# A two-layer decoder whose five engine queues are laid in a new order

## The reference, cut to what matters

```python
x = _layernorm(x + _L0_attn_ref(x, ...))           # a Mamba block: conv, silu, selective scan, gate
x = _layernorm(x + _L0_xattn_ref(x, ctx_768, ...)) # cosine similarity of two projections, 256 x 256
x = _layernorm(x + _L0_ffn_ref(x, ...))            # top-2 of 4 experts, low-rank additions to one MLP
x = _layernorm(x + _L1_attn_ref(x, ...))           # 16 heads, 4 key/value heads, rotary, softmax
x = _layernorm(x + _L1_xattn_ref(x, ctx_768, ...)) # one-head attention on the context
x = _layernorm(x + _L1_ffn_ref(x, ...))            # a gated recurrence over the 8 batches in turn
```

```python
h = dAt * h + dBxt                     # per batch, channel (512) and state (16), over 256 positions
y = jnp.einsum('bdn,bn->bd', h, Ct)
```

## Time and profile before

| | us |
|---|---|
| median of 3 runs | 1197.41 |
| lowest and highest | 1194.89, 1200.62 |
| the profiled execution | 1199.11 |
| span of its instructions | 1197.2 |

### The profile page before, as it was taken

The page is one execution under the profiler, slowest core; times in us unless marked ns, Lnnn a source line. Parts: engine busy times, 40 slices in busy tenths (PEclk is TensorE's granted clock), DMA queues, the critical chain, the costliest instruction groups (busy, mean ns, idle before and its releaser), DMA issues.

```text
span 1197.2 us, 17415 instructions
## 1 busy us (share of the span) xinstructions
PE 1083.9 (91%) x6154; PEld 794.0 (66%) x6154; DVE 1009.7 (84%) x1690; ACT 763.3 (64%) x2010; POOL 209.2 (17%) x257
## 2 busy tenths in 40 slices
PE   5666789899999999999998999999999999999984
...
DVE  3899999999999999999999999999998994333316
...
PEclk8766779999999999999999999999998999999997
...
GB/s 224 145 35 135 42 44 52 68 39 72 71 92 89 63 81 71 119 63 71 80 104 63 32 102 78 116 33 91 85 120 36 63 62 31 1 1 10 125 15 70
DMA packets 41193, 86.70 MB, mean 72 GB/s; under 512 B 3737, under 2 KB 14970, under 8 KB 40466
## 3 DMA queue, kind: packets, MB, share of 16 engines
...
## 4 chain that ended last, share of the span: by engine, by line
PE 67%; DVE 19%; issue 5%; ACT 5%; POOL 3%; DMA 1%; ACTq 0%; DVEq 0%; SPq 0%; POOLq 0%
PE bank L301 20%; DVE scans L598 5%; PE bank L716 5%; PE bank L1306 4%; PE bank L764 4%; PE bank L1344 4%; PE bank L1315 4%; PE bank L982 4%; PE bank L1355 3%; PE bank L974 3%; PE bank L532 3%; PE bank L1244 3%; DVE scans L606 2%; PE bank L1338 2%; PE bank L295 2%
## 5 line engine op out<-in xcount | busy, mean ns | idle before, releaser
L561 ACT ACTIVATE scans<-dt,a_neg 128x255 f32<-128x255 f32 x512 | 224.6, 501 | 0.1
L632 POOL DMA_DIRECT2D scans<-scans x96 | 84.6, 881 | 441.6 <-DVE scans L606 441.3
L606 DVE TENSOR_TENSOR scans<-scans,BC 128x1024 f32<-128x1024 f32 x128 | 155.9, 1218 | 0.2
L598 DVE TENSOR_TENSOR_SCAN scans<-scans 128x1024 f32<-128x1024 f32 x64 | 146.1, 2282 | 6.0 <-ACT scans L561 6.0
L598 DVE TENSOR_TENSOR_SCAN scans<-scans,dBx_odd 128x1024 f32<-128x1024 f32 x64 | 146.2, 2284 | 3.0 <-ACT scans L561 2.8
L1392 ACT ACTIVATE ya<-bank,nmax 128x256 f32<-128x256 f32 x240 | 110.7, 473 | 34.2 <-DVE nmax L1459 18.3
L532 PE MATMUL bank<-ident,scans 128*128 128x128 f32 x640 | 101.4, 296 | 18.0 <-DVE scans L606 17.7
L1459 DVE TENSOR_REDUCE nmax<-bank 128x2 f32<-128x512 f32 x128 | 84.3, 683 | 36.4 <-PE bank L1306 35.9
L532 PEld LDWEIGHTS bank<-ident,scans 128*128 128x128 f32 x640 | 82.5, 153 | 37.6 <-DVE scans L606 21.9
L1401 ACT ACTIVATE ya<-bank 128x512 f32<-128x512 f32 x120 | 68.6, 604 | 21.2 <-PE bank L1315 20.6
L1306 PE MATMUL bank<-kT,qT 64*128 64x256 f32 x512 | 72.3, 402 | 5.8 <-ACT ya L1401 4.5
...
## 6 DMA issues: line engine op xcount, KB each, us to landing
...
```

The source lines that it names most:

```text
L561: ins = act.activation(step[:, j, 1:S], dt[b % 2][:, c, 1:S], ACT.Exp, scale=a_neg[:, c, n:n + 1])
L598: dve.tensor_tensor_scan(H, H, flat(dBx[u % 2]), 0.0, ALU.mult, ALU.add).then_inc(s["a_scan"], 1)
L606: dve.tensor_tensor(H, H, Ch, ALU.mult).then_inc(s["a_hC"], 1)
```

## The change

Only the letters of `ORDER` change. Every engine keeps the same steps and each stream its own order, so the instructions, their operands and their semaphores are the same. The new strings come from a model of the queues in which a GpSimd instruction also waits for work with two SBUF operands that VectorE begins shortly behind it. How far the steps move: of DVE's 1294 steps 527 keep their place and 922 are within one place of it; of PE's 1245, 588 and 988; of ACT's 1155, 428 and 767; of POOL's 165 all but one are within one place, and of SP's 89 all but seven. The largest moves are two steps on ACT that come 36 and 44 places earlier. Of the pairs of DVE steps whose order turns round, 105 put an S step ahead of a W step and 84 one ahead of a Y step; 37 and 61 do the reverse.

In the start, DVE's order `F13 F14 S6 F15 S7 F16 S8 S9` becomes `F13 S6 F14 S7 F15 S8 F16 S9`. On ACT the two normalisations F16 and F17 stood ahead of S8 and now stand behind S9, and S10 to S15 are laid between F17 and F21. On PE, S4 and S5 now stand ahead of the turn F11, and W0 (four products) and S6 between F12 and F13. DVE's F17 moves from its 35th place to its 42nd. The step W5 of DVE (L1615 to L1617) stood ahead of S48 and now stands behind G1, so that G0 and G1 come before it.

In the middle, seven turns of a layernorm on PE (L295) now have other steps of PE ahead of them that stood behind:

| turn at, us | idle before it, us | now ahead of it |
|---|---|---|
| 266.84 | 0.40 | L1338 and L1344 (and L301 behind it) |
| 324.40 | 1.18 | L301 |
| 383.85 | 0.99 | L1306 |
| 476.35 | 1.43 | L1244, L532 |
| 635.44 | 0.66 | L1315, L301 |
| 653.82 | 0.24 | L1338, L1344, L532 |
| 900.01 | 1.60 | L1344 |

On SP, the load of batch 6's context for the second layer (`cz`, L946) moves from ahead of three loads of the scan's B and C (L501, `BC`) to behind them. PE's queue is the same from its 1190th step on.

```diff
     "pe": (
-        "FFFFFFFFFFSWFSSSFSFFYSYFFWSSSSYYSFSFSSFSYWSSSWGGGGSSFYSSWWWWWWYYSSYYWYWSWFSWFWWWFSYWWWWWYWWWWFFWWSWWWWYWWWWWSF"
-        "YYSWFYSYYYYSYYYYFYYSYYYSYYFYYSYSVYYGGVGGYSVSFYVFYWWWFYWWVSWVYSYYFFWVWYVYSYWVYVFWYSWWWYWVWFVYWYSWWYWVWSVWWFWSWY"
...
+        "FFFFFFFFFFSFSSSSSFFYWSFWYSSSFFSYSSFSSFYSSYWFSYGGGWGSSSFWWWYWSWYWYSSYWYSWSFWYFFWSWWWWWWSWWWWYWWFWWYFWWWWWSWWWWY"
+        "FYSFYSYYYYWYYYYFSYYYSYYFYYSYYYSSVVGGGYYGYFVVSFYYFWWWYWWSWVSYVYSYVVFWFYWYYWSYVYVWFSWWWYWVVWYSYWFWWYWWVSVWWFWWSW"
...
     "act": (
-        "FFFFFFFFFFFFFSSFSSSFFSSSFFSFSFFFSSSSSSFSSFFSSFSSSSSSFFSSSSSSSSGGWFSSSSSSGGWSWWSFSWWSWSWSFFFFSWSWSSWFFWWWSWFFSW"
...
+        "FFFFFFFFFFFFFSSFFSSSFSSSSSFFSSSFSFSFSFSSSSFSFFSSSSSFSSSSSSFFSSSGSGFWSSSGGSWWWSFSSSSSWWWSWFFSFFSSFWWFSWSWWSWWWF"
...
     "dve": (
-        "FFFFFFFFFFFFSWWSSSFSSFFSFSFSSSSSWSFSFYSFSSSSSSSFSYSSFSFSFSSSFSYWYSSSSSSSSSSSWSSSSFSWSGGSSGSGGFSGSGSGWSSYSSWYSS"
-        "WYWWSWYWWFYSSSWWWFWFWFWWSYWSWWYWSSSSWFYFSWSYFWSSSWFSSFSFYWFWFWSWYWYWSSSSSYYYSSSYSFYSSYSSFYYSSFSYYFYGGSFSYSSGFG"
...
+        "FFFFFFFFFFFWWFSSSFSSSFSFSFSFSSSSSSSSSYSSSFSSSFSSSWFSYSSFSFSFWSFFSSSSSYSSSSSSSSSFSWYSGGYWSGSGGFGSGSGWSSSSSSWYSS"
+        "WYWYWYWSWWFFSSSWFWFWYWYWSWSWSWWSWSWSYSSWFSSWFSWFSWSSFSYFWFFWFWYWYWWSSYSSSYYYSSYSFSFYSSYSSSYYSFFSYFYFSGGYSSGSGG"
...
     "pool": (
-        "FFGWWFWFGSSWWSSSSSSSSWWVSSSSWSSSSGFSWWSSSSSWWSVSSSSWSSSSSGFSWSWSSSSSSWWVSSSWSSSSSGSWSFWSSSSSSWWVSSSSWSSSGSSFWS"
-        "WSSSSSSWWSVSSSWSSSGSSWWSSSSSSSWWVSSSSWSSGWWWWVWWVWWWWWW"
+        "FFGWWFWFGSSWWSSSSSSSWSWVSSSSWSSSGSSFWWSSSSSSWWVSSSSWSSSSSGFSWSWSSSSSSWWVSSSWSSSSSGSWSFWSSSSSSWWVSSSWSSSSSGSFWS"
+        "WSSSSSSWWSVSSSWSSSGSSWWSSSSSSSWWSVSSSWSSGWWWWVWWVWWWWWW"
...
     "sp": (
-        "WFSFWSSFWSWGWSSFSFFWGSSSFFSSGWWWSWSSFFSGWWWWSSSFFSGWWWSSFWSSWGFWWSSFWSSWGWWWSSSGWWWWWWWWW"
+        "WFSFWSSWFSWGSFWSWSFFSGSSFFSSGWWWWSSFFSSWGWWSWSFSSFWGWWSSFSWSGFWWWWSSFSSGWWWSSSWGWWWWWWWWW"
```

More of the change, by code:

```diff
@@ L52 @@
[L52 to L56, removed]
@@ new lines @@
+        "FVYSWWWYFYFYVWVWWWWYYWWSYWSWYFWWVVWWFSWWYWWWWWWWSWWVVVVVVVVVSVYSFWYYWWYWYYWWYSWWYYWYSWYYSWYSWYWYWWWYWWSWWYWSYW"
+        "VYFSVWWGYYGGYGVVSYYSSSVYWVWWYYWYWWVFWVYSYFFYVVYWSYWYFFVVWWYYWWWYVWWVFWSYYWWFVVWWVSVWWVWWVWSWWWWWWWVWSVVVFSYWYY"
+        "SWWYWYYYWWSYWYWYYWYWSSYWWYWYWWWYSWWWWWSYYWVYSWWVGYGYGGYVVSSYSWFYWSWWYVVWYYWYVWVYSYYSVVFWYYWYFFWVVWYYSWWWWFWFWV"
+        "YVWWYSYWWVVWWSVFWWVFWVWWWSWWWWWVVVVSVYFYWSYWWYWYYWWYSWWYYYSWYWYYSWWYWYWWYWSWWWWWYSYWSWWGYVGGVGYYSSSFWYVVWWYWYY"
+        "SWWVWYVYSYVVFFFWYYWYVVSYWYSVYWFFWWWWVYWWYSWWVYVWWFWYWYSVVVWWVWWWFWSWWWWWSVVVVVVSYFWYYYWYWYSYWYWWYYWWYSWYWYSYWW"
@@ L59 @@
+        "WYWWSWWWYWWSWWSYWGWYGGGYSSWSFWVVWYWSYWYWWVVYYSYVVWWYWYSVYWVWWYWSWYWWYVVWSWYYWWYWWYVVWSYWWYWWWWVVYYWSWWWVVVVVSV"
+        "VVSVWVYWWYSYYYWYYYWWYSWWYYWSYWYWYYWSWYWWWWWWWWYSYWWSYVGGWGGVYYWYWWWVVYYWYWWVVYYYVVWYYWYVVWYYWVYVWWWWYYWWVYVWWY"
+        "YWWVVWWVVWWVWWWWWWWWWVVVVVYWYYYYYYYYYYWWYYWYYWYWYWYWYVVYWYYWVVYYWWYWVYYWWWWYVYWYWYVVYYYWWWWYVVWVVYYYVVYVVVVVVV"
         "WVVVWWWWWWWWWWWWWWWWWWWWWWWWWWWWWWW"
@@ L66 @@
[L66 to L70, removed]
@@ new lines @@
+        "WWWYWYVSYYFFSWFYWYWYYWSFVYSSWWVFYWSWYWSYSSFVSWWSSWWYWWSVVWWWSWWWWYSSWYWYWSSSSYYWWFWYWYSSWYSSYWYSYSYWSSYWGVYYGW"
+        "FYWYVYYGSGSWYYWYVYWWSFFYSYFYFSVYFSFYWWYWYYVWYFFYFSWSVYYFWWVYYWSYSFYWFWVSWSWSWSSSWWWWYSWWSVVWWWWSWYSWSWSYFYWWYW"
+        "YSSSSWWWYYWSWSYWYSYYSWYWWYGSYGSWYVYYGVGWSSYWYFSWWSYYYYVYYVYYSSFFYWWYWYYFFVWYFFSYWYSYVWWSFFSWYVYWYYFWFSSVWSFWWS"
+        "FSSWWSYWWFSWWVSVWWWWWSWWSYYSWWWSSYYYSWWYWSYWWSYSWWYSSWYWYGGWYSVYYSYSSWGGFYWYYVYWWSYYFSYVYSFYSFVFYWWWYYFWFYYVSY"
+        "YSWFYWFWSYWSVYFYWFYWYVSSYYFSWVWSWSSFSSWWWWYWWVVSSWWWFSWWYYSWWYWWYWSSYSWYWWSSWWYSWWSYYSWGSSWWGYYWGGSWYSYVWWYYSS"
@@ L73 @@
+        "FYYYYVSSWWWYYWYVYSSWWYYWVYYWSSYYVWYYWSYSWYVYYWSSWYYYVSSYVSSWWWWSWWSYWVVWWWSSWYWWYSWWYWYSYWWYSYWSWYWWYYYWGGWWWY"
+        "YYYGGWVWYYWWYYVYYVYYWYWYWYYVWYYVYYWYWYVWYYWYVYWYYWWWWVWWWWYVWWYYYYWVWYWWWYYYWWYYYYYWWVWYYYYVWWYYYYWYYYWWYVYYYY"
+        "YVYYYWWWVYYWWVYYYVYVWWWWWVVWWWWWWWWWWWWWWWWWWWWWWWWWWWW"
     ),
     "dve": (
-        "FFFFFFFFFFFFSWWSSSFSSFFSFSFSSSSSWSFSFYSFSSSSSSSFSYSSFSFSFSSSFSYWYSSSSSSSSSSSWSSSSFSWSGGSSGSGGFSGSGSGWSSYSSWYSS"
-        "WYWWSWYWWFYSSSWWWFWFWFWWSYWSWWYWSSSSWFYFSWSYFWSSSWFSSFSFYWFWFWSWYWYWSSSSSYYYSSSYSFYSSYSSFYYSSFSYYFYGGSFSYSSGFG"
@@ L77 @@
[L77 to L81, removed]
@@ new lines @@
+        "WYWYWYWSWWFFSSSWFWFWYWYWSWSWSWWSWSWSYSSWFSSWFSWFSWSSFSYFWFFWFWYWYWWSSYSSSYYYSSYSFSFYSSYSSSYYSFFSYFYFSGGYSSGSGG"
+        "VGYGYGYSSSYSFSYWVFYWSWFWWVWYWYYSSSWFWYWFWVWFWYWYWFWFWYWSSSSVYYSWSSSWYVSSWSYYSWFSSYWSWVSWSWSWVWWWWVFVSVVVVSVSVY"
+        "YSYSSSSWSYSSSYWWWWWWWYSSSYSYFSYSWSSYGYSGSSSGGYVGGYGYFGWFYVWFSYSYSSSWYVYYWWWWVWYWSSFYFFYWWWSWWWWWWWYVWSYFFYFFWS"
+        "WYYFSSVYSSVWYSWSSSSSWSWWWWWVWFWWSVSVVVVVSVSVYSYYSSSSWSSWYWSWWWYWSWYSSSSSYSYSSYFSSYYSGGSYSWSGVYFGGYGWGWGFVYFSYY"
+        "SFSYSYSWVSYWWYWSWVWYWFYFSFSWVWYWYWWWWYWWFWYWFSFFVFSYYWSSWYVSSSSVWFSWSSSSSWSWWVWVWWWWWVVVSVSSVYVYSYSSSSYSWSSYWW"
```

23 lines of the change are left out of this document (9 added, 14 removed).

## The result

The changed kernel takes 1187.94 us (median of 5 runs, 1187.36 to 1190.96); the kernel before takes 1197.33 beside it. The ratio is 0.9926, with a 95% interval of 0.9904 to 0.9947. The execution profiled took 1190.96 us, with a span of 1189.1.

A forecast was written before the change was run, and what follows sets the result against it. VectorE was taken to be full in the start and TensorE to bound the rest; only idle times change. Start -4 and middle -3 from 1199.11 us profiled give 1192.1, 1190.5 on the median; 8-in-10 range 1179 to 1206.

The forecast's parts named there:

- a middle that begins no earlier: Sign of being wrong: the middle, after batch 0's start, would not begin earlier; the forecast had it 4 us earlier.
- VectorE's two old stops: Batch 0's start: the 3.24 us stop before scan L598 and 1.06 us before L448 both go, -4.3 us.
- What is late next: Start, behind GpSimd's shift: F17 can begin near 68.4 us, giving VectorE one new stop of 1.4 us, bounds 0 and 2.5.
- The gate: Gate after batch 0's scan: W5 fills the time TensorE works on the gate; -1.1 us, between 0 and -2.7.
- The middle, what is cured: Seven turns (L295) that stopped TensorE get other work ahead, -6.5 us; the 2.44 us at 578 us stay.
- The middle, what is new: Middle: new stops made by the new interleaving, 3.5 us, between nothing and 9 us.
- The end and the other queues: End in the same order, 0; GpSimd at most 1 us if its cover is gone; SyncE's moved load costs nothing.
- Nothing comes of it: Rival, 1197.4 us: F17's new stop takes back most of 4.3 us, the middle makes as many stops as cured; chance 0.27.
- the form by the rule: Form of the no-effect rival: GpSimd instructions begun first are never held, so covers guard against nothing; 1197.4 us, chance 0.04.
- Slower: Rival, attention of batches 1 to 6: scans ahead delay maxima or statistics, eight stops of 2.2 us; 1204.5 us, chance 0.21.
- Better: Rival, 1182 us: GpSimd not held at 48 us, gate's gain whole, no new middle stops, few smaller cures; chance 0.07.

The follow-up runs named there:

- inearly: Changed kernel with batch 0's start partly put back: F18 to F21 earlier on ScalarE, F13 ahead of Y0 on TensorE; 1185.25 us, ratio 0.9891.
- best: startold with seven steps of batch 0's start moved: S8 to S11 earlier on ScalarE, S14 to S16 ahead of F17 on VectorE; 1179.39 us, ratio 0.9854.
- startold: Order of the kernel before up to the turn of batch 0's MLP norm, the changed kernel's order from there; 1185.28 us, ratio 0.9887.
- gateold: Changed kernel with the old order from the end of batch 0's scan to the turn of its MLP norm; 1189.43 us, ratio 0.9917.
- turns: Kernel before with eight norm turns on TensorE alone put behind the steps the new order puts ahead of them; 1201.61 us, ratio 1.0024.
- dve5: Kernel before with five small exchanges on VectorE alone, so norm shifts avoid the scan that held them; 1191.91 us, ratio 0.9943.
- noshift_old: Kernel before with GpSimd's shift (L285) of each norm left out, so part of the computation is missing; 1178.23 us, ratio 0.9834.

## Why the prediction was right, and where it was wrong

The time was nearly right (1190.5 predicted, 1187.94 measured) by luck, since two errors cancelled: -4 and -3 were predicted for the start and the middle, +6.65 and -14.69 came. One of the prediction's own signs of being wrong, a middle that begins no earlier, came true: it begins 6.65 us later.

**VectorE's two old stops (-4.3 us).** Half right. The 3.24 us before L598 fell to 0.65. The 1.06 us before L448 did not go; that stop grew.

**What is late next (+1.4, bounds 0 and 2.5).** This step failed, and the sign of the start with it. Two stops came, 3.25 + 2.65 = 5.9 us. The shift ended at 54.94 and not at 53.7, since both of GpSimd's operations were held (3.73 and 3.88). From there to F17 it was 17.4 us and not 14.7, and F17 came at 72.3 and not at 68.4. The sum (7.1 + ScalarE's six steps + W0 and S6) had both of its new terms wrong. Between F12 and F13 TensorE did other work for 7.0 us (62.40 to 69.36), not 2: W0 and S6 took 3.78 + 1.54, where I took "about 1 us" each for eight matmuls at the low clock, and Y0 with its 2.07 us had been forgotten, which stood behind F13 and now stands ahead of it (the list of the change leaves it out too). ScalarE's six steps, put at 5.6 us, lay mostly beside TensorE's work: F12 began 5.46 us behind the shift's end and not 3.77 as before, so 1.7 us of them counted there, and the step between F20 and F21 cost less than 1. VectorE's arrival (66.4 to 67) doesn't follow from its own terms, as three and a half units of 4.5 us from 53.5 give 69.2; what it did until F17 was less, 12.3 us beside its stops. And I called Y0's stop "part of the same one". It stands ahead of F17 in VectorE's queue and waits for another product, and scan steps lie between them, so both count. "inearly" and "best" show that these places cost the time: put back or moved less, they give 2.7 and, against startold, 2.1 us.

**The gate (-1.1, bounds 0 and -2.7).** Wrong sign: the scan of batch 0 ended 1.2 us later, the rest of the first part took 5.4 more. Moving W5 did not fill TensorE's time, because TensorE came to S17 (L532) only at 127.80, behind F18 (L301, 3.76 us), and VectorE stood 3.71 us before L613, ahead of W5. "gateold" gives 3.55 us back. I had excluded a loss without a reason.

**The middle, what is cured (-6.5).** Wrong in its mechanism. I credited the steps put ahead of seven turns on TensorE; "turns" has these and gains nothing. A cure is on VectorE, where the scan begins behind the shift ("dve5", 6.6 us by five exchanges), and what there was to win was what the shifts cost in the old order, 13 to 18.5 us ("noshift_old"), not the 6.5 of the stops that I had listed. How the rest of the new middle's gain splits between the strings of the five engines is not shown. That also explains the 2.44 us at 578, of which I said that they stay because nothing passes that turn: the shift there fell from 2.22 us to 0.20. And I priced idle time alone, while 6.6 us of the gain stand in TensorE's busy time, 1.5 of them in the turns themselves.

**The middle, what is new (+3.5).** About right: the waits other than those before L295 grew by 3.0 us (30.74 - 12.63 = 18.11, now 22.65 - 1.56 = 21.09).

**The end and the other queues (0).** Right: 69.63 and 69.57 us.

**The rivals.** "Nothing comes of it" is excluded: the middle gained 14.69 us, and "noshift_old" and "dve5" show that the holds cost time. But neither tests the form by the rule that an operation begun first is never held, and its premise was wrong: most of the long holds of the kernel before are of shifts that began just behind VectorE's scan (574.52 behind 574.47, 471.56 behind 471.52, 897.06 behind 897.05), and these the rule has as well. Where GpSimd began first, by 0.10 us, that rule of the Trainium skill (SBUF — State Buffer, Who interferes with whom) disagrees with the measurement here. "Slower": each new stop was under 2.1 us, and the net growth was 3 and not 17.6. "Better" didn't come either: GpSimd was held at 47 us as before and the start lost, while the middle gained 6 us more than the 8.5 of that case.
